# Spreading the gates of a mixture of twelve experts over the partitions: by a product on TensorE, or by DMA through DRAM

## The reference, cut to what matters

```python
dw1 = _route_dense(x_addr @ U1.T, K, TAU)      # (1024, 12), three non-zero in each row
dw2 = _route_dense(x_addr @ U2.T, K, TAU)
dw3 = _route_dense(x_addr @ U3.T, K, TAU)
h = _apply_mixture(x_flat, dw1, W1)            # sum over e of (x @ W1[e].T) * dw1[:, e:e+1], 512 wide
h = jax.nn.gelu(h, approximate=False)
y = _apply_mixture(h, dw2, W2)
y = y + dw3 @ b2
```

## Time and profile before

| | before |
|---|---|
| median of 3 runs | 504.03 us (503.49 to 505.67) |
| the profiled execution | 503.41 us, span 501.7 us |
| mean granted TensorE clock | 0.962 |
| PE busy | 450.8 us (90%) |
| PEld busy | 327.8 us (65%) |
| DVE busy | 321.8 us (64%) |
| ACT busy | 187.4 us (37%) |
| POOL busy | 241.8 us (48%) |
| queue of SP's DMAs | 14.25 MB, 12.3% of 16 DMA engines' span |

### The profile page before, as it was taken

How to read it: one execution, slowest core, us unless ns; L and a number is a source line. 1 busy time by engine, 2 the same in 40 slices (tenths; PEclk the granted TensorE clock), 3 DMA queues, 4 the chain that set the end, 5 groups by cost and what they waited for, 6 DMA issues and landing times.

```text
span 501.7 us, 8554 instructions
## 1 busy us (share of the span) xinstructions
PE 450.8 (90%) x3282; PEld 327.8 (65%) x3282; DVE 321.8 (64%) x686; ACT 187.4 (37%) x290; POOL 241.8 (48%) x209
## 2 busy tenths in 40 slices
PE   2982968988799999999999999588999999999997
PEld 1761746656466676667677667266667777888885
DVE  8952695999976756765769866834463533275454
ACT  5744435454444545543544544112334532300000
POOL 7441344789577776787678748224333333000000
PEclk9997887999899999999999999788999999999999
DMA  7359500000000000000000020010222110000000
GB/s 171 116 104 99 130 2 1 2 0 1 0 1 1 2 1 1 1 1 0 1 2 2 2 87 1 21 43 22 65 63 64 63 64 21 2 6 12 10 5 12
DMA packets 31658, 15.08 MB, mean 30 GB/s; under 512 B 16077, under 2 KB 29314, under 8 KB 31618
## 3 DMA queue, kind: packets, MB, share of 16 engines
q1 hardware_dynamic: 30916, 14.25, 12.3%
q10 hardware_dynamic: 702, 0.28, 0.2%
HBM read 12.56 MB, written 1.97 MB: 29 GB/s over the span
## 4 chain that ended last, share of the span: by engine, by line
PE 70%; DVE 16%; issue 4%; ACT 4%; DMA 3%; POOL 2%; SPq 1%; DVEq 0%; ACTq 0%; POOLq 0%
PE psum L1044 9%; PE psum L1027 9%; PE psum L847 7%; PE psum L1175 5%; PE psum L1212 4%; PE psum L1211 4%; PE psum L1213 4%; PE psum L1177 4%; PE psum L1176 4%; DVE xn L1255 3%; PE psum L1063 3%; PE psum L950 2%; PE psum L1078 2%; PE psum L1054 2%; DVE rden L1428 2%
## 5 line engine op out<-in xcount | busy, mean ns | idle before, releaser
L465 POOL TENSOR_TENSOR e_part<-e_sb 128x512 f32<-128x512 f32 x64 | 91.0, 1439 | 39.8 <-DVE e_sb L1421 39.8
L703 ACT ACTIVATE e_sb<-psum 128x1024 f32<-128x1024 f32 x64 | 62.2, 1023 | 15.6 <-PE psum L1027 15.5
L1027 PE MATMUL psum<-q_t,kT 64*128 64x256 f32 x512 | 64.8, 392 | 0.3 <-ACT e_sb L703 0.3
L1044 PE MATMUL psum<-e_sb,v_sb 128*64 128x256 f32 x512 | 63.7, 392 | 0.0
L497 POOL TENSOR_TENSOR xeT_lo<-xeT,xeT_hi 128x512 fp32r<-128x512 f32 x24 | 30.9, 1290 | 67.0 <-ACT xeT_hi L717 67.0
L1428 DVE RECIPROCAL rden<-psum 128x256 f32<-128x256 f32 x32 | 56.0, 1749 | 2.1 <-PE psum L1054 2.0
L457 POOL TENSOR_TENSOR k_rot<-rope_a,rope_b 128x512 f32<-128x512 f32 x32 | 41.3, 1291 | 32.8 <-DVE rope_b L1317 32.8
L1596 DVE SCALAR_TENSOR_TENSOR x_sb<-psum,dw,x_sb 128x128 f32<-128x128 f32 x96 | 33.7, 351 | 34.8 <-PE psum L1213 32.2
L685 ACT ACTIVATE kT<-psum 128x512 f32<-128x512 f32 x32 | 19.2, 599 | 94.5 <-PE psum L950 94.3
L1027 PEld LDWEIGHTS psum<-q_t,kT 64*128 64x128 f32 x512 | 47.3, 188 | 10.9 <-issue 5.2
L1421 DVE TENSOR_SCALAR e_sb<-e_sb 128x1024 f32<-128x1024 f32 x64 | 47.7, 781 | 7.5 <-ACT e_sb L703 7.5
(11 more groups left out here) (189 smaller groups left out, 793.2 us busy)
## 6 DMA issues: line engine op xcount, KB each, us to landing
w_raw<-in_L_ffn_W_dram SPq DMA_DIRECT2D x24, 256.0 KB, 2.7
ctx_sb<-in_ctx_dram SPq DMA_DIRECT2D x4, 256.0 KB, 5.7
bd_dram<-bd_raw SPq DMA_DIRECT2D x4, 206.2 KB
bd<-bd_dram SPq DMA_DIRECT2D x8, 99.0 KB
vbd<-v_dram SPq DMA_DIRECT2D x8, 79.7 KB
v_dram<-v_tok SPq DMA_DIRECT2D x4, 136.0 KB, 2.2
vbd<-v_dram SPq DMA_DIRECT2D x8, 65.3 KB
raw<-in_L_xattn_Wkv_dram SPq DMA_DIRECT2D x2, 256.0 KB, 5.4
```

The lines of the kernel that those rows point to most:

```text
L465: pool.tensor_tensor(e_part[:, p % 2, half, :, :], e_sb[:, i % ERING, :, 0, :], e_sb[:, i % ERING, :, 1, :], ALU.add)\
L703: act.activation(e_sb[:, i % ERING, :, :, :].rearrange("p a k t -> p (a k t)"), psum[:, a:a + 2, :].rearrange("p a b -> p (a b)"), ACT.Exp ...
L1027: mm = pe.matmul(psum[:, 2 * (i % 2) + a, t * S:(t + 1) * S], kT[rows, p % 3, kt * P:(kt + 1) * P], q_t[rows, j % 2, p % 2, :], start=True ...
L1044: mm = pe.matmul(psum[DX * a:DX * a + DX, pv_bank(p), 0:S], v_sb[g % 2][:, kt, 2 * pp + a, :], e_sb[:, i % ERING, a, t, :], start=(kt == 0 ...
```

## The change

Only the experts 0, 1 and 2 of each half (GE = 3) keep the spreading product. For the other nine, in each half, the gates are written to a DRAM tensor of 12 rows by 512 and read back three rows at a time to all 128 partitions: six loads of 128 x 3 x 512 floats (768 KB written to SBUF, from 6 KB of DRAM), into two buffers `gates`. The loads stand in SP's program ahead of the weight loads of steps 4, 10, 14, 16 and 20. For it ACT copies the turned gates a second time, unrounded, to `gate_src` (12 x 512), after DVE has taken the rest; the transposes of the bias gates in step 9 and the spreading product of n = 1 now wait for that copy, since it reads their bank. `dw1T` holds one half in place of two, `spread` three experts in place of twelve, and the spreading products use bank 4 + n % 2 in place of 5 - n % 2.

```diff
+    GE = 3
+    GLOADS = [(half, q) for half in range(2) for q in range(1, NE // GE)]
+    GATE_AT = {4: (0, 1), 10: (2,), 14: (3,), 16: (4,), 20: (5,)}
...
+        gate_dram = nc.dram_tensor("gate_dram", [2, NE, 4 * P], F32, kind="Internal").ap()
...
-        spread = sb("spread", [SPLIT, NE, P], F32R, third)
+        spread = sb("spread", [SPLIT, GE, P], F32R, third)
+        gate_src = sb("gate_src", [NE, 4 * P], F32, third)
+        gates = sb("gates", [P, 2, GE, 4 * P], F32, third)
...
-        dw1T = sb("dw1T", [SPLIT, 2, 4 * P], F32R, third)
+        dw1T = sb("dw1T", [SPLIT, 4 * P], F32R, third)
...
+            def store_gates(half):
+
+                sp.wait_ge(s["gate_src_done"], half + 1)
+                sp.dma_start(gate_dram[half], gate_src[:, :]).then_inc(s["gate_stored"], 16)
+                sp.wait_ge(s["gate_stored"], 16 * (half + 1))
+
+            def load_gates(g):
+
+                half, q = GLOADS[g]
+                if g >= 2:
+                    before, last = GLOADS[g - 2]
+                    sp.wait_ge(s["xe_done"], before * NE + (last + 1) * GE)
+                rows = gate_dram[half, q * GE:(q + 1) * GE].rearrange("e t -> (e t)")
+                sp.dma_start(gates[:, g % 2, :, :].rearrange("p e t -> p (e t)"), rows.partition_broadcast(P)).then_inc(s[f"ld_gate{g % 2}"], 16)
+
             for n in range(2 * NE):
+                for g in GATE_AT.get(n, ()):
+                    if GLOADS[g][1] == 1:
+                        store_gates(GLOADS[g][0])
+                    load_gates(g)
...
-                    act.activation(dw1T[0:NE, half, :], bank(at, NE), ACT.Copy).then_inc(s["dw1_hi_done"], 1)
+                    act.activation(dw1T[0:NE, :], bank(at, NE), ACT.Copy).then_inc(s["dw1_hi_done"], 1)
+                    act.wait_ge(s["dw1_lo_done"], half + 1)
+                    if half:
+                        act.wait_ge(s["gate_stored"], 16)
+                    act.activation(gate_src[:, :], bank(at, NE), ACT.Copy).then_inc(s["gate_src_done"], 1)
...
             def spread_weights(n):
 
                 half, e = divmod(n, NE)
+                if e >= GE:
+                    return
                 pe.wait_ge(s["dw1_lo_done"], half + 1)
                 if n == 0:
                     pe.wait_ge(s["spread_done"], 1)
+                    pe.wait_ge(s["ox_done"], NPAIR - 1)
                 elif n == 1:
-                    pe.wait_ge(s["ox_done"], NPAIR - 1)
+                    pe.wait_ge(s["gate_src_done"], 1)
                 else:
                     pe.wait_ge(s["xe_done"], n - 1)
-                pe.matmul(bank(5 - n % 2), spread[:, e, :], dw1T[:, half, :], start=True, stop=True).then_inc(s["spread_ps"], 1)
+                pe.matmul(bank(4 + n % 2), spread[:, e, :], dw1T[:, :], start=True, stop=True).then_inc(s["spread_ps"], 1)
...
-                        pe.wait_ge(s["dw1_lo_done"], 2)
+                        pe.wait_ge(s["gate_src_done"], 2)
...
             def expert_tokens(n):
 
-                dve.wait_ge(s["spread_ps"], n + 1)
+                half, e = divmod(n, NE)
                 if n >= 2:
                     dve.wait_ge(s["xeT_lo_done"], n - 1)
-                dve.tensor_tensor(xeT[:, n % 2, :], bank(5 - n % 2), xnT[:, n // NE, :], ALU.mult).then_inc(s["xe_done"], 1)
+                if e < GE:
+                    dve.wait_ge(s["spread_ps"], half * GE + e + 1)
+                    gate = bank(4 + n % 2)
+                else:
+                    g = GLOADS.index((half, e // GE))
+                    dve.wait_ge(s[f"ld_gate{g % 2}"], 16 * (g // 2 + 1))
+                    gate = gates[:, g % 2, e % GE, :]
+                dve.tensor_tensor(xeT[:, n % 2, :], gate, xnT[:, half, :], ALU.mult).then_inc(s["xe_done"], 1)
```

More of the change, by code:

```diff
@@ L251, in decoder_layer @@
             z_done fill_done top_done top3_done zr_done chosen_done zsh_done ez_done wsel_done zsum_done zrec_done
-            dw_done pick_done spread_done dw1_ps dw1_hi_done dw1_lo_done dw3_ps dw3_done spread_ps xe_done
+            dw_done pick_done spread_done gate_src_done gate_stored ld_gate0 ld_gate1 dw1_ps dw1_hi_done dw1_lo_done dw3_ps dw3_done spread_ps xe_done
             xeT_hi_done xeT_lo_done h_ps h_f_done h_hi_done h_lo_done y_ps y_done bias_ps bias_done x3_done""".split()
@@ L521, in _ @@
                     pool.memset(top3[:, :, TOPK:8], LOWEST).then_inc(s["fill_done"], 1)
-                    pool.memset(dw1T[:, :, :].bitcast(F32), 0.0).then_inc(s["fill_done"], 1)
+                    pool.memset(dw1T[:, :].bitcast(F32), 0.0).then_inc(s["fill_done"], 1)
                     pool.tensor_tensor(pick[:, :], ident[0:SPLIT, 0:NE], ident[0:SPLIT, REST:SPLIT], ALU.add).then_inc(s["pick_done"], 1)
                     pool.wait_ge(s["pick_done"], 1)
-                    pool.tensor_copy(spread[:, :, :], pick[:, :, None].to_broadcast([SPLIT, NE, P])).then_inc(s["spread_done"], 1)
+                    pool.tensor_copy(spread[:, :, :], pick[:, 0:GE, None].to_broadcast([SPLIT, GE, P])).then_inc(s["spread_done"], 1)
             token_rest(0)
@@ L1483, in route @@
                     dve.wait_ge(s["dw1_hi_done"], half + 1)
-                    dve.tensor_tensor(dw1T[REST:SPLIT, half, :], bank(at, NE), dw1T[0:NE, half, :].bitcast(F32), ALU.subtract)\
+                    dve.tensor_tensor(dw1T[REST:SPLIT, :], bank(at, NE), dw1T[0:NE, :].bitcast(F32), ALU.subtract)\
                        .then_inc(s["dw1_lo_done"], 1)
```

## The result

The changed kernel took 497.14 us (median of 4 runs, 495.86 to 498.30) against 503.76 us for the kernel before: a ratio of 0.9863, with a 95% interval from 0.9825 to 0.9901. Timed again in another group it was 497.57 us, ratio 0.9871 (0.9856 to 0.9886). The prediction was 497.4 us in a range of 494.8 to 501.0. Two single executions of the study, one of the kernel before (1089.61 us) and the profiled one of the kernel before with the parts of h moved (737.56 us), are in none of the ratios.

The account below looks back on a forecast made before the run. PE was taken to bound nearly the whole first mixture. Terms: -9.7 + 1.0 + 0.5 + 0.2 + 1.4 = -6.6 us from 503.41 gives 496.8, plus 0.6 for the median: 497.4 us, range 494.8 to 501.0.

Parts of the forecast that it names:

- The mechanism: First mixture: PE sets the end, so spreading products leaving its queue shorten the span until another chain is as long.
- The price of a product: PE's steps: 3.78 us between experts with a product, 3.21 without, so 0.57 each, 17 of them 9.7 us.
- the lower bound: PE's steps: a product is worth only its own slot, 17 x 0.43 = 7.3 us.
- The entry: Half 0, ahead of expert 0: ACT's second copy delays the weights and all behind them, +1.0 us.
- the branch of +0.5: Expert 0: the clock rises at the same moment as before, so half of the copy's microsecond comes back.
- Steps 5 to 9: Routing of half 1: products worth 1.71 us gain 1.2, 0.5 lost waiting for dw; step 9's copy loses 0.2.
- Steps 13 to 15: After expert 11: ACT's and DVE's fixed order lets PE gain 0.3 of 1.71 us; 1.4 lost.
- The loads: Gate loads of 768 KB: taken to land in 8 us, load 2 wanted some 12 after issue; hidden, cost nothing.
- The rival of late loads: From load 2, issued in step 4, wanted in step 7: late loads cost 9 us at 16 us landing; 5%.
- The shared side: xeT on two SBUF tensors: every one waits for POOL, 1.76 in place of 0.69 us, time 503; 12%.
- The clock: New waits, up to 1.0 us in step 8, 0.5 in 14 and 15: clock falls, 499 to 501; 8%.
- The range's upper end: Whole kernel: 501 us, from bounds of a product's price (+2.4) and the copy's delay ahead of expert 0 (+1.7).

Follow-up runs that it names:

- the control on the kernel before: Kernel before with the parts of h of half 0 taken one chunk at a time in steps 14, 16, 18 and 20: 503.65 us, ratio 0.9991.
- the version with all three moves: Changed kernel with second copy behind first weights, h's parts in steps 14, 16, 18, 20, and half 1's routing pulled apart: 494.85 us, ratio 0.9819.

## Why the prediction was right

Its terms against the profiles, each as a difference between distances (before to after), in the order of the steps:

| term | predicted | measured |
|---|---|---|
| expert 0 behind the transposes of the gates: 5.99 to 6.83 us | +1.0 | +0.84 |
| the same at expert 1: 18.51 to 18.97 us (19.14 in the second profile) | +1.0 | +0.46 to +0.63 |
| expert 1 to the transposes of step 5, four products: 19.23 to 16.95 us | -2.28 | -2.28 |
| from there to the gates' transposes of half 1: 13.52 to 12.39 us | -1.2 | -1.13 |
| from there to the transposes of the bias gates: 4.20 to 3.80 us | -0.4 | -0.40 |
| transposes of step 12 to those of step 15: 11.34 to 11.18 us | -0.3 | -0.16 |
| transposes of step 15 to those of step 22: 25.95 to 22.36 us | -3.4 | -3.59 |

- **The mechanism**, products that leave the queue of the engine that sets the steps, was right: put back unread, they take the gain away.
- **The price of a product**, read from the one step that had none, was right to 0.02 us: 3.21 was predicted for a step, 3.19 to 3.2 measured. That it is 0.57 and not its slot of 0.43 was right too: the lower bound would have made four products 1.7 us instead of 2.3.
- **The entry.** The copy costs 0.84 us (shown by moving it). The prediction took the whole as lost and named the rise of the clock as the open point. In order of time the matmuls of expert 0 stand 0.43 us apart at the low clock and 0.23 at the high one; the change from one to the other came 2.9 us behind its first matmul before, and 2.1 and 2.5 us behind it in the two profiles of the changed kernel. So less of expert 0 lies under the low clock, and from expert 0 to expert 1 it is 12.1 to 12.3 us instead of 12.5: 0.2 to 0.4 us come back. This is the larger part of the 0.3 to 0.6 us by which the sum was too small, and it is the branch of +0.5 that the prediction named and did not take. Behind the transposes of the gates the change came at 8.7 to 9.1 us before, in the changed kernel and with the copy moved, though expert 0 began at 5.99, 6.83 and 5.99; in the second profile it came at 9.1 to 9.4. So it did not follow expert 0 in these four profiles. What sets it was not tested.
- **Steps 5 to 9**, right in size: a wait of 0.54 us for dw, as forecast, and one of 0.27 for the weights of the same step that was not named. Shown for the first by pulling the routing apart. In step 9 the copy ended at 373.04 and the transposes of the bias gates began at 373.09, 3.80 behind those of the gates.
- **Steps 13 to 15**, right in mechanism; the gain there is 0.16 instead of 0.3 us. DVE's chain kept its time exactly: the low part of step 14's weights ended 11.03 us behind the transposes of step 12 before (400.43 against 389.40) and after (396.64 against 385.61). But the transposes begin 0.15 us behind that end (396.79), and the prediction had let them begin at it. That h's parts hold the chain is shown by moving them; the control on the kernel before agrees within its interval. A wait of 0.19 us in step 13 was not named and stayed.
- **The loads** are hidden, with more room than thought: 4.4 us to landing where 8 had been taken. Three times a weight load was too much: if both kinds of load lay on one line, 2.8 us for 256 KB and 4.4 for 768 KB would leave a part of 2.0 us that does not grow with size, an estimate, and the prediction counted it three times. The estimate from the Trainium skill (DMA: Bandwidth & Descriptors, Anatomy of one DMA), 3.8 us, was nearer; the trace has 4.0 at least. The rival of late loads is real, but not at this place of the loads: three steps of delay made one load late, and the fallen clock then added to the wait, which the rival's price had left out.
- **The shared side** did not decide. Of the 18 xeT one took 1.74 us, in step 1, where POOL's low part of expert 2 had just begun; the others 0.68 to 0.80. The same place in the kernel before, with the gate in PSUM, had 0.69 us (POOL and DVE, before and then after):

```profile
339.81 1.28 POOL L497 TENSOR_TENSOR xeT_lo<-xeT,xeT_hi 128x512 fp32r<-128x512 f32 x1
339.95 0.69 DVE L1453 TENSOR_TENSOR xeT<-psum,xnT 128x512 f32<-128x512 f32 x1 [2.77 <-POOL xeT_lo L497]
```

```profile
339.85 1.27 POOL L522 TENSOR_TENSOR xeT_lo<-xeT,xeT_hi 128x512 fp32r<-128x512 f32 x1
339.93 1.74 DVE L1492 TENSOR_TENSOR xeT<-gates,xnT 128x512 f32<-128x512 f32 x1 [2.71 <-POOL xeT_lo L522]
```

PE waited for it only in the version with all three moves, 0.74 us in step 2. The rival's price, a full 1.07 us for each, was too high even with POOL made busy.
- **The clock** did not fall in the new waits of up to 0.54 us.

The median came out 0.3 us under the forecast. The medians differ by 503.76 - 497.14 = 6.6 us, the forecast to the tenth, and that is luck: by the profiles the change took off 6.9 to 7.2 us, and single executions of one kernel scatter by more than 2 us. The range's upper end is not quite the sum of its own terms, which gives 497.4 + 2.4 + 1.7 = 501.5 and not 501.0; nothing hung on it.

## What to carry to other kernels

When PE sets the steps, price an instruction of its queue by the distance between its neighbours with and without it, not by its own slot, and then ask at each place which chain is next: here 2.3 us of 9.7 were lost between steps 5 and 15, nearly all of it where the work that was taken out had covered another chain. Such places show before the change as chains that end a few tenths of a microsecond ahead of the engine that waits for nothing. Moving one of them, the parts of h, was worth 1.2 us in the new kernel and nothing that could be told in the old one. A transfer that replaces computation has a deadline rather than a price as long as it is hidden: here a single late one cost nearly the whole gain.

## What the runs showed of the hardware

- A broadcast of 6 KB of DRAM to 128 partitions (768 KB) landed in 4.0 to 4.6 us in nine of twelve loads of the two profiles of the changed kernel. Two took 6.8 us, each issued directly behind another such load. One took 6.5 us, behind a weight load issued 0.4 us before it, where another in the same position took 4.2, so its cause stays open.
- After a wait of 4.64 us PE ran at the lower of its two clocks for some 6 us, and the following step was 2.4 us longer; after waits of 0.54 and 0.40 us, and of 1.31 us with more work on POOL, it stayed at a granted clock of 1.00. A wait alone does not tell which: the same wait of 3.39 us ahead of expert 1 was followed by the lower clock in the changed kernel and not in the version with all three moves.
- A DVE operation on two SBUF tensors waits for the POOL operation in progress, up to 1.1 us, but not for the next in POOL's queue, which becomes longer instead (1.50 against 1.04 us). With one operand in PSUM it took 0.69 us beside the same POOL operation. The Trainium skill (GPSIMD Engine Reference, Key points) names the contention with DVE instructions that have two SBUF inputs; the traces agree, and give its length.
